# Landmark attention layer: four batch loops against one row of 32 tile slots

## The chip, the cores and the metric

The kernel runs on one core of one Trainium2 chip. The metric is the device time of one execution in microseconds (us). The engines that matter are PE (TensorE, the matrix multiplier), DVE (VectorE), ACT (ScalarE), Pool (GpSimd) and SP (SyncE, which here only issues transfers). Each runs its own instruction list in order; semaphores order them against each other. PEld is the loading of weights into TensorE.

## The reference, cut to what matters

The program computes eight residual layers on x, which has 4 batches of 1024 rows of 128 features: each layer adds f(layernorm(x)) to x. Only the third, the landmark attention, is touched:

```python
def _L0_attn_b_ref(hidden_states, Wq, bq, Wk, bk, Wv, bv):
    L = 64
    q = softmax(hidden_states @ Wq + bq);  k = softmax(hidden_states @ Wk + bk)
    v = hidden_states @ Wv + bv
    k_landmarks = k.reshape(B, L, S // L, D).mean(axis=2)
    kernel_1 = einsum('bqd,bkd->bqk', q, k_landmarks)
    kernel_2 = einsum('bkd,bld->bkl', k_landmarks, k)
    mid = einsum('bkl,bld->bkd', kernel_2, k * v)
    return einsum('bqk,bkd->bqd', kernel_1, mid)
```

The kernel regroups these products. With lm the 64 x 128 landmarks and M = sum over rows of k^T (k * v), a 128 x 128 matrix, the output is q (lm^T lm) M. So a batch needs two sums over its rows (M and lm), then the square lm^T lm, then its product with M, and then q times that.

## The kernel before, in words

`landmark_layer` (lines 827 to 1023) holds x in SBUF (`g.X`, 32 tiles of 128 rows) with the mean and variance of each row (`g.MV`), which the layer before left there. A batch is 8 tiles; a chunk is 4 tiles. All data are f32. The layer opens with three weight and three bias transfers, a square root and reciprocal for the layernorm, and a matrix product that spreads the three biases over all partitions (L914), copied to SBUF by DVE (L971).

Each batch is one call of `sequence` on each engine; three calls are a hardware loop (`Fori`), the fourth is written out. In it:

- PE turns the normalised rows of a chunk (L920); ACT copies them to `xt` (L886). For each tile PE makes q, k and v in one product of 384 columns into one of four PSUM banks (L933). DVE adds the biases in place (L984) and takes the row maxima of q and k (L985). ACT makes both exponentials with their sums (L895, L896). DVE takes the reciprocals of the sums (L990), scales k into `kk` (L992) and makes `k3`, that is k times v (L993). PE adds to M (L938) and to lm (L939) and turns the exponential of q (L944); after four tiles ACT copies the turned ones (L899).
- On PE, tile t's L933 stands ahead of tile t-2's L938, L939 and L944. On DVE, tile t's L984 and L985 stand ahead of tile t-1's L990, L992 and L993.
- At a batch's end, with no tile work of the next one issued yet: DVE copies lm and M (L996, L997), normalises the first chunk of the next batch (L113, four instructions), copies the square (L1001) and the middle product (L1003), adds the eight output tiles to x (L1010), normalises the second chunk, and measures the new x (L122, L125, and a copy of the statistics at L127). PE meanwhile makes the square (L946), turns a chunk, makes the middle product (L950), the eight output tiles in two banks (L955) and turns the second chunk. ACT copies the two turned chunks.

Pool only makes the averaging matrix at the start of this layer. SP has nothing to do after the six transfers. The layers are separated by a barrier of all engines.

## Time and profile before

| | us |
|---|---|
| median of 3 runs | 2824.74 |
| lowest and highest run | 2817.64, 2830.39 |
| the profiled execution: its own time | 2821.07 |
| the profiled execution: span of its trace | 2819.1 |

In that execution PE is busy for 80% of the span, DVE 65%, ACT 51% and Pool 31%, over all eight layers; its mean granted TensorE clock is 0.865 of full speed. The landmark layer is the short stretch from 391.9 to 519.8 us.

How to read the rows further down. Times are us unless marked ns. A row of stretches gives start:end and length, then the busy us (and number of instructions) of PE, PEld, DVE, ACT and Pool in this order, the granted TensorE clock as a share of full speed (0.50 is 1.2 GHz, 1.00 is 2.4 GHz), the share of the DMA engines and the GB/s. A row of a timeline gives the start, the time from the start of the first to the end of the last instruction merged in it, the engine and line, what it writes and reads, shapes and count, and in brackets how long the engine had been idle and what released it. A row of a group gives count, busy us, the mean ns of one, and the idle time ahead of them with its releaser. A line is a line of the kernel before. An f32 matrix product shows as two PE records.

### The profile page before, as it was taken

The page shows a single profiled execution, that of the slowest core. Times are in us where ns is not written, and L with a number is a line of the kernel's source. Part 1 is how long each engine was busy: PE and PEld are TensorE (multiplying, and loading weights), DVE is VectorE, ACT ScalarE, POOL GpSimd, SP SyncE. Part 2 cuts the span into 40 slices and gives each one's busy share as a digit, 9 for nine tenths or more (in the row PEclk, how much of TensorE's full clock was granted, in tenths as well). Part 3 has the DMA queues.
Part 4 walks back from the last instruction along what each step waited for, and adds up shares of the span by engine and source line. Part 5 has one row for each costly group of instructions (what it writes and reads, how often), then busy time and mean ns, then how long its engine had stood idle before and what let it go on. Part 6 is the DMA issues. An engine that isn't in the chain of part 4 may idle for free. (4 is left out here: it accounts for less than half of the span.)

```text
span 2819.1 us, 79607 instructions
## 1 busy us (share of the span) xinstructions
PE 2250.5 (80%) x30676; PEld 1640.9 (58%) x30676; DVE 1820.5 (65%) x5861; ACT 1425.0 (51%) x3583; POOL 865.8 (31%) x852
## 2 busy tenths in 40 slices
PE   6489947589934888798888877948888888888786
PEld 3389924479921333333333337936777777777686
DVE  5533356633335777777777633359999999999533
ACT  4366632366621445445454544635555555555264
POOL 2157620057741100000000002624444444443255
PEclk8589977689965898989989886969999999999688
DMA  3011120011135211111110001121111111111113
GB/s 123 30 38 49 47 68 0 30 35 49 48 126 153 74 32 35 29 30 35 33 43 18 18 3 47 46 84 50 51 50 49 48 50 45 48 48 47 41 39 90
DMA packets 81721, 139.72 MB, mean 50 GB/s; under 512 B 18691, under 2 KB 37803, under 8 KB 78924
## 3 DMA queue, kind: packets, MB, share of 16 engines
q1 hardware_dynamic: 62244, 101.88, 11.6%
q0 software_dynamic: 13824, 28.34, 3.5%
...
q14 instruction: 115, 0.94, 0.1%
...
## 5 line engine op out<-in xcount | busy, mean ns | idle before, releaser
L1353 ACT ACTIVATE ca_pt<-ca_ps 128x512 f32<-128x512 f32 (+3 forms) x768 | 341.1, 491 | 369.6 <-PE ca_ps L1445 168.2
L668 PE MATMUL ffn_ps<-ffn_xst,ffn_up_w 128*128 128x128 f32 x3456 | 430.0, 279 | 0.2 <-issue 0.2
L668 PEld LDWEIGHTS ffn_ps<-ffn_xst,ffn_up_w 128*128 128x128 f32 x3456 | 411.8, 196 | 1.2 <-issue 1.2
L782 DVE TENSOR_TENSOR ffn_hid<-ffn_sg,ffn_ps 128x512 f32<-128x512 f32 x216 | 148.5, 688 | 363.1 <-PE ffn_ps L668 360.2
L540 POOL DMA_INDIRECT ffn_xs<-ffn_x,ffn_token_at x216 | 209.1, 968 | 256.7 <-DVE ffn_token_at L765 192.1
L1419 PE MATMUL ca_ps<-ca_stacks 72*128 72x512 bf16 (+3 forms) x768 | 230.1, 367 | 64.9 <-DVE ca_m_near L1567 31.3
L1774 POOL TENSOR_TENSOR im_pt_e<-im_pt,im_own 128x512 f32<-128x512 f32 x128 | 162.6, 1270 | 384.9 <-DVE im_pt L2027 367.0
L1441 PE MATMUL ca_ps<-ca_stacks 75*128 75x512 bf16 (+3 forms) x768 | 254.0, 354 | 19.2 <-ACT ca_pt L1353 11.2
L1566 DVE TENSOR_REDUCE ca_m_far<-ca_ps 128x1 f32<-128x128 f32 (+5 forms) x384 | 236.6, 616 | 47.1 <-PE ca_ps L1419 45.5
L545 POOL DMA_INDIRECT ffn_y<-ffn_ys,ffn_result_at x216 | 212.6, 984 | 153.7 <-DVE ffn_ys L788 146.1
L1567 DVE CUSTOM_DVE_ANT_0 ca_spill<-ca_ps,ca_bias_q 128x256 f32<-128x256 f32 (+1 forms) x512 | 200.7, 397 | 35.8 <-PE ca_ps L1419 35.8
L1463 PE MATMUL ca_ps<-ca_pt,ca_vp 128*9 128x512 f32 (+3 forms) x1536 | 181.9, 548 | 43.2 <-ACT ca_ysb L1361 43.2
L509 POOL MEMSET ffn_later<- 128x128 f32 x4 | 0.8, 206 | 697.0 <-POOLq L42 697.0
L1781 POOL TENSOR_TENSOR im_rope_qk<-im_t,im_mates 128x512 f32<-128x512 f32 x128 | 170.6, 1333 | 56.8 <-DMA im_mates<-im_t 56.0
L1419 PEld LDWEIGHTS ca_ps<-ca_stacks 72*128 72x128 bf16 x768 | 67.9, 103 | 199.6 <-DVE ca_m_near L1567 100.2
L1580 DVE TENSOR_TENSOR ca_ps<-ca_ps,ca_bias_kd 128x256 f32<-128x256 f32 (+1 forms) x288 | 109.8, 382 | 98.1 <-PE ca_ps L1441 94.6
L1807 ACT ACTIVATE im_ot<-im_ps 128x256 f32<-128x256 f32 x128 | 49.1, 383 | 241.4 <-PE im_ps L1870 241.4
L598 ACT ACTIVATE ffn_up_w<-w_w 128x1024 f32 x144 | 151.9, 1056 | 29.3 <-issue 26.8
L1441 PEld LDWEIGHTS ca_ps<-ca_stacks 75*128 75x128 bf16 x768 | 78.9, 103 | 146.2 <-ACT ca_pt L1353 71.9
L591 ACT ACTIVATE ffn_sg<-ffn_ps 128x512 f32<-128x512 f32 x216 | 128.9, 597 | 59.9 <-PE ffn_ps L668 59.8
L1821 ACT ACTIVATE im_pe_<-im_s,im_nm 128x32 f32<-128x32 f32 x512 | 157.0, 316 | 1.9 <-DVE im_nm L2036 1.9
L676 PE MATMUL ffn_ps<-w_w,ffn_hid 128*128 x1152 | 152.4, 276 | 1.2 <-DVE ffn_ys L788 1.2
...
## 6 DMA issues: line engine op xcount, KB each, us to landing
im_mates<-im_t SPq DMA_DIRECT2D x256, 128.0 KB
...
```

The source lines that it names most:

```text
L540: nc.gpsimd.indirect_dma_start(out=xs[:, n % XS, :], out_offset=None, in_=xn_rows[:, :], in_offset=bass.IndirectOffsetOnAxis(ap=token_at[: ...
L545: nc.gpsimd.indirect_dma_start(out=y_rows[:, :], out_offset=bass.IndirectOffsetOnAxis(ap=result_at[:, n:n + 1], axis=0), in_=ys[:, n % YS, ...
L668: last = nc.tensor.matmul(ps[:, bank, j * P:j * P + P], up_w[:, n % WS, first + j * P:first + j * P + P], xst[:, n % 2, :], start=True, st ...
L1353: nc.scalar.activation(pt[:, i % 8, lo - c0:hi - c0], ps[:, tile_bank(i), lo - c0:hi - c0], ACT.Exp, scale=SCALE).then_inc(p_ready, 1)
L1419: last = nc.tensor.matmul(slot_row(n)[:, c:e], stacks[0:KD, u % 3, 0, j, qt * P:qt * P + P], stacks[0:KD, u % 3, 1, j, c:e], start=True, s ...
L1441: last = nc.tensor.matmul(ps[:, tile_bank(i), lo - c0:hi - c0], stacks[:, u % 3, 1, j, kt * P:kt * P + P], stacks[:, u % 3, 0, j, lo:hi], ...
L1463: nc.tensor.matmul(ps[32 * j:32 * j + D + 1, 7, lo - c0:hi - c0], vp[:, b % 2, kt, gr * G4 + j, :], pt[:, i % 8, lo - c0:hi - c0], start=( ...
L1566: nc.vector.tensor_reduce(m_far[:, u % 2, t:t + 1], slot_row(n)[:, 0:lo], AX_X, ALU.max)
L1567: nc.vector.tensor_tensor_reduce(spill[:, n % 2, 0:hi - lo], slot_row(n)[:, lo:hi], bias_q[:, h, W2 - (hi - lo):W2], 1.0, NEG, ALU.add, AL ...
L1774: nc.gpsimd.tensor_tensor(pt_e[:, j % 2], pt[:].unsqueeze(2).to_broadcast(shape), own[:].unsqueeze(1).to_broadcast(shape), ALU.mult).then_ ...
L1781: nc.gpsimd.tensor_tensor(rope_qk[:, k % 2].rearrange("p a b -> p (a b)"), t1[:], mates[:, k % 2, :], ALU.subtract).then_inc(S["rope_ready ...
L1821: last = nc.scalar.activation(pe_[:, h, :], s1[:, h, :], ACT.Exp, bias=nm[:, h:h + 1], accum_out=sm[:, j % 2, h:h + 1])
```

## The change

The layer becomes one row of 32 tile slots over all four batches, then ten more slots without new tiles. No engine has a hardware loop left in it: everything is written out.

- The work of a batch's end is spread over slots of the next batch. With x the slot's number within a batch, PE: turn the odd chunk at x=1 and the next even one at x=2, square at 3, middle product at 4, first four output tiles at 5, last four at 7. DVE: copies of lm and M at 2, of the square at 3, of the middle product at 4, first four additions to x at 6 and their statistics at 7, the last four at x=0 of the batch after and their statistics at 1. The last batch's end runs in the ten slots without tiles.
- `kk` (L992) goes from DVE to Pool, for all 32 tiles. M's and lm's products now wait for both `k3` from DVE and `kk` from Pool.
- Normalised rows: the first three chunks on DVE at the start, the other 20 tiles on Pool, one after each `kk`.
- Turned x goes through the bank of the output (`ps_o`) and no longer through the bank of the turned exponentials (`ps_t`). Both halves of the output use `ps_o`, so the second waits until the first is added. M and lm share a bank, one bank for each parity of the batch; `xt`, `eqt`, `lm`, `mm`, `aa` and `nn` are doubled, `xn` holds four chunks.
- The spread of the biases no longer waits for the averaging matrix, and the first rows no longer wait for the spread. The statistics are written straight into `g.MV`.

The diff, without the removed lines (they are in the functions above), the declarations of semaphores and unchanged lines; "..." marks what is left out, and eight leading blanks of each line are cut:

```diff
+AHEAD = 3
...
+std, RS = s.sb("std", [P, NT]), s.sb("rstd", [P, NT])
+xn = s.sb("xn", [P, 4, CT, P])
 w = s.sb("w", [P, 3, P])
...
+xt = s.sb("xt", [P, 2, 2, CHUNK])
+nmx, sums, rs = s.sb("nmx", [P, NT, 2]), s.sb("sums", [P, NT, 2]), s.sb("rs", [P, NT, 2])
...
+eqt = s.sb("eqt", [P, 2, TB, P])
+lm, mm, aa, nn = s.sb("lm", [LM, 2, P]), s.sb("mm", [P, 2, P]), s.sb("aa", [P, 2, P]), s.sb("nn", [P, 2, P])
...
 ps_t, ps_qkv, ps_o = s.ps("ps_t", [P, CT, P]), s.ps("ps_qkv", [P, 4, 512]), s.ps("ps_o", [P, CT, P])
...
+ps_sum = s.ps("ps_sum", [P, 2, 512])
...
 mm_ready, a_done, a_ready, n_done, n_ready = (s.sem(n) for n in ("mm_ready", "a_done", "a_ready", "n_done", "n_ready"))
...
+TURN_ODD, TURN_EVEN, MEAN, SQUARE, MIDDLE, OUT0, OUT1 = 1, 2, 2, 3, 4, 5, 7
+def after_slot(n):
+    return n // TB, n % TB
 with nc.Block() as block:
     @block.sync
...
     @block.gpsimd
     def _(pool):
...
+        pool.wait_ge(rstd_ready, 1)
+        pool.wait_ge(xn_ready, AHEAD)
+        def row(n):
+            c, k = n // CT, n % CT
+            if k == 0 and c >= 4:
+                pool.wait_ge(turned, c - 3)
+            last = nc.gpsimd.tensor_scalar(xn[:, c % 4, k, :], g.X[:, n, :], g.MV[:, n, 0:1], RS[:, n:n + 1], ALU.subtract, ALU.mult)
+            if k == CT - 1:
+                last.then_inc(xn_ready, 1)
+        for n in range(NT):
+            pool.wait_ge(rs_ready, n + 1)
+            if n >= 4:
+                pool.wait_ge(summed, n - 3)
+            nc.gpsimd.tensor_scalar(kk[:, n % 4, :], ek[:, n % 4, :], rs[:, n, 1:2], None, ALU.mult).then_inc(kk_ready, 1)
+            if AHEAD * CT + n < NT:
+                row(AHEAD * CT + n)
     @block.scalar
     def _(act):
...
+        nc.scalar.activation(std[:], g.MV[:, :, 1], ACT.Sqrt, bias=g.eps[:, 0:1]).then_inc(std_ready, 1)
+        def copy_xt(c):
+            act.wait_ge(turned, c + 1)
+            nc.scalar.activation(xt[:, c // 2 % 2, c % 2, :], ps_o[:].rearrange("p a b -> p (a b)"), ACT.Copy).then_inc(xt_ready, 1)
+        def exps(n):
+            act.wait_ge(mx_ready, n + 1)
+            if n >= 4:
+                act.wait_ge(summed, n - 3)
+                act.wait_ge(k3_ready, n - 3)
+            nc.scalar.activation(ek[:, n % 4, :], ps_qkv[:, n % 4, P:2 * P], ACT.Exp, bias=nmx[:, n, 1:2], accum_out=sums[:, n, 1:2])
+            nc.scalar.activation(eq[:, n % 4, :], ps_qkv[:, n % 4, 0:P], ACT.Exp, bias=nmx[:, n, 0:1], accum_out=sums[:, n, 0:1]).then_inc(exp_ready, 1)
+        def copy_eqt(k):
+            b, h = k // 2, k % 2
+            act.wait_ge(summed, k * CT + CT)
+            if b >= 2:
+                act.wait_ge(o_ready, 2 * b - 2)
+            nc.scalar.activation(eqt[:, b % 2, h * CT:h * CT + CT, :], ps_t[:], ACT.Copy).then_inc(eqt_ready, 1)
+        copy_xt(0)
+        for n in range(NT + 2):
+            q, x = after_slot(n)
+            if n < NT:
+                exps(n)
+            if n % CT == 1 and n > CT:
+                copy_eqt(n // CT - 1)
+            if x == TURN_ODD and 2 * q + 1 < NC_:
+                copy_xt(2 * q + 1)
+            if x == TURN_EVEN and 2 * q + 2 < NC_:
+                copy_xt(2 * q + 2)
     @block.tensor
     def _(pe):
+        def turn(c):
+            pe.wait_ge(xn_ready, c + 1)
+            for k in range(CT):
+                last = nc.tensor.transpose(ps_o[:, k, :], xn[:, c % 4, k, :], g.ident[:])
+            last.then_inc(turned, 1)
+        def project(n):
+            b, t = n // TB, n % TB
+            if t % CT == 0:
+                pe.wait_ge(xt_ready, 2 * b + t // CT + 1)
+            if n >= 4:
+                pe.wait_ge(k3_ready, n - 3)
+                pe.wait_ge(exp_ready, n - 3)
+            nc.tensor.matmul(ps_qkv[:, n % 4, 0:3 * P], xt[:, b % 2, t // CT, t % CT * P:t % CT * P + P], w[:].rearrange("p a b -> p (a b)"),
+                             start=True, stop=True).then_inc(qkv_ready, 1)
+        def sum_tile(n):
+            b, t = n // TB, n % TB
+            bank = ps_sum[:, b % 2, :]
+            if t == 0 and b >= 2:
+                pe.wait_ge(mm_ready, b - 1)
+            pe.wait_ge(k3_ready, n + 1)
+            pe.wait_ge(kk_ready, n + 1)
+            nc.tensor.matmul(bank[:, 0:P], kk[:, n % 4, :], k3[:, n % 4, :], start=(t == 0), stop=(t == TB - 1), skip_group_check=True)
+            nc.tensor.matmul(bank[0:LM, P:2 * P], avg[:, WIN - PER * t:WIN - PER * t + LM], kk[:, n % 4, :],
+                             start=False, stop=(t == TB - 1), skip_group_check=True)
+            pe.wait_ge(exp_ready, n + 1)
+            if n % CT == 0 and n:
+                pe.wait_ge(eqt_ready, n // CT)
+            nc.tensor.transpose(ps_t[:, n % CT, :], eq[:, n % 4, :], g.ident[:]).then_inc(summed, 1)
+        def square(b):
+            pe.wait_ge(mm_ready, b + 1)
+            if 2 * b + 4 < NC_:
+                pe.wait_ge(xt_ready, 2 * b + 5)
+            elif 2 * b + 3 < NC_:
+                pe.wait_ge(xt_ready, 2 * b + 4)
+            else:
+                pe.wait_ge(x_added, 2 * b)
+            nc.tensor.matmul(ps_o[:, 0, :], lm[:, b % 2, :], lm[:, b % 2, :], start=True, stop=True).then_inc(a_done, 1)
+        def middle(b):
+            pe.wait_ge(a_ready, b + 1)
+            nc.tensor.matmul(ps_o[:, 1, :], aa[:, b % 2, :], mm[:, b % 2, :], start=True, stop=True).then_inc(n_done, 1)
+        def output(b, h):
+            if h == 0:
+                pe.wait_ge(n_ready, b + 1)
+            else:
+                pe.wait_ge(x_added, 2 * b + 1)
+            pe.wait_ge(eqt_ready, 2 * b + h + 1)
+            for k in range(CT):
+                last = nc.tensor.matmul(ps_o[:, k, :], eqt[:, b % 2, h * CT + k, :], nn[:, b % 2, :], start=True, stop=True)
+            last.then_inc(o_ready, 1)
         pe.wait_ge(loaded, 16 * 6)
+        nc.tensor.matmul(ps_sum[:, 1, 0:3 * P], g.ones[0:1, :], brow[:].rearrange("p a b -> p (a b)"), start=True, stop=True).then_inc(spread, 1)
+        turn(0)
...
+        for n in range(NT + TB):
+            q, x = after_slot(n)
+            if n < NT:
+                project(n)
+            if 2 <= n < NT + 2:
+                sum_tile(n - 2)
+            if x == TURN_ODD and 2 * q + 1 < NC_:
+                if q >= 2:
+                    pe.wait_ge(x_added, 2 * q - 2)
+                else:
+                    pe.wait_ge(xt_ready, 2 * q + 1)
+                turn(2 * q + 1)
+            if x == TURN_EVEN and 2 * q + 2 < NC_:
+                pe.wait_ge(xt_ready, 2 * q + 2)
+                turn(2 * q + 2)
+            if q:
+                if x == SQUARE:
+                    square(q - 1)
+                if x == MIDDLE:
+                    middle(q - 1)
+                if x == OUT0:
+                    output(q - 1, 0)
+                if x == OUT1:
+                    output(q - 1, 1)
     @block.vector
     def _(dve):
...
+        dve.wait_ge(std_ready, 1)
+        nc.vector.reciprocal(RS[:], std[:]).then_inc(rstd_ready, 1)
+        dve.wait_ge(rstd_ready, 1)
+        for c in range(AHEAD):
+            for k in range(CT):
+                n = c * CT + k
+                last = nc.vector.tensor_scalar(xn[:, c, k, :], g.X[:, n, :], g.MV[:, n, 0:1], RS[:, n:n + 1], ALU.subtract, ALU.mult)
+            last.then_inc(xn_ready, 1)
+            if c == 0:
+                dve.wait_ge(spread, 1)
+                nc.vector.tensor_copy(bias[:], ps_sum[:, 1, 0:3 * P]).then_inc(spread, 1)
+        dve.wait_ge(spread, 2)
+        def add_bias(n):
+            dve.wait_ge(qkv_ready, n + 1)
+            out = ps_qkv[:, n % 4, 0:3 * P]
+            nc.vector.tensor_tensor(out, out, bias[:], ALU.add).then_inc(biased, 1)
+            dve.wait_ge(biased, n + 1)
+            nc.vector.tensor_reduce(nmx[:, n, :], ps_qkv[:, n % 4, 0:2 * P].rearrange("p (a b) -> p a b", a=2),
+                                    AX_X, ALU.max, negate=True).then_inc(mx_ready, 1)
+        def weigh(n):
+            dve.wait_ge(exp_ready, n + 1)
+            nc.vector.reciprocal(rs[:, n, :], sums[:, n, :]).then_inc(rs_ready, 1)
+            if n >= 4:
+                dve.wait_ge(summed, n - 3)
+            dve.wait_ge(rs_ready, n + 1)
+            nc.vector.scalar_tensor_tensor(k3[:, n % 4, :], ek[:, n % 4, :], rs[:, n, 1:2], ps_qkv[:, n % 4, 2 * P:3 * P],
+                                           ALU.mult, ALU.mult).then_inc(k3_ready, 1)
+        def copy_sums(b):
+            dve.wait_ge(summed, b * TB + TB)
+            nc.vector.tensor_copy(lm[:, b % 2, :], ps_sum[0:LM, b % 2, P:2 * P])
+            nc.vector.tensor_copy(mm[:, b % 2, :], ps_sum[:, b % 2, 0:P]).then_inc(mm_ready, 1)
+        def copy_square(b):
             dve.wait_ge(a_done, b + 1)
...
+            nc.vector.tensor_copy(aa[:, b % 2, :], ps_o[:, 0, :]).then_inc(a_ready, 1)
+        def copy_middle(b):
             dve.wait_ge(n_done, b + 1)
...
+            nc.vector.tensor_copy(nn[:, b % 2, :], ps_o[:, 1, :]).then_inc(n_ready, 1)
+        def add_output(c):
+            dve.wait_ge(o_ready, c + 1)
+            for k in range(CT):
+                n = c * CT + k
+                last = nc.vector.scalar_tensor_tensor(g.X[:, n, :], ps_o[:, k, :], rs[:, n, 0:1], g.X[:, n, :], ALU.mult, ALU.add)
+            last.then_inc(x_added, 1)
+        def new_stats(c):
+            hold(dve, x_added, c + 1)
+            for k in range(CT):
+                last = nc.vector.bn_stats(raw[:, c % 2, k, :], g.X[:, c * CT + k, :])
+            last.then_inc(raw_ready, 1)
+            hold(dve, raw_ready, c + 1)
+            for k in range(CT):
+                nc.vector.bn_aggr(g.MV[:, c * CT + k, :], raw[:, c % 2, k, :])
+        for n in range(NT + TB + 2):
+            q, x = after_slot(n)
+            if n < NT:
+                add_bias(n)
+            if 1 <= n < NT + 1:
+                weigh(n - 1)
+            if q:
+                if x == MEAN:
+                    copy_sums(q - 1)
+                if x == SQUARE:
+                    copy_square(q - 1)
+                if x == MIDDLE:
+                    copy_middle(q - 1)
+                if x == OUT0 + 1:
+                    add_output(2 * q - 2)
+                if x == OUT1:
+                    new_stats(2 * q - 2)
+                if x == 0 and q >= 2:
+                    add_output(2 * q - 3)
+                if x == 1 and q >= 2:
+                    new_stats(2 * q - 3)
 s.clear()
```

## Rows read from the trace of the kernel before

**Rows 1.** Busy time by stretch of this layer: opening, then eight-tile runs and batch ends alternating
```profile
391.90:403.30 11.40, 5.13 (x13) 3.04 (x14) 3.05 (x10) 3.45 (x5) 0.75 (x3) 0.50 0.06 17
403.30:418.40 15.10, 12.93 (x49) 6.28 (x48) 12.67 (x40) 7.56 (x34) 0.00 (x0) 0.94 0.00 1
418.40:431.90 13.50, 9.35 (x39) 6.80 (x39) 8.02 (x38) 3.07 (x4) 0.00 (x0) 0.76 0.00 1
431.90:449.00 17.10, 13.67 (x52) 7.14 (x50) 12.57 (x40) 6.93 (x33) 0.00 (x0) 0.89 0.00 0
449.00:462.40 13.40, 9.33 (x37) 6.26 (x35) 8.02 (x38) 3.07 (x4) 0.00 (x0) 0.77 0.00 0
462.40:478.40 16.00, 12.11 (x46) 6.40 (x45) 12.57 (x40) 6.95 (x33) 0.00 (x0) 0.87 0.00 0
478.40:493.10 14.70, 10.94 (x40) 7.79 (x39) 8.02 (x38) 1.79 (x3) 0.00 (x0) 0.67 0.00 0
493.10:509.50 16.40, 12.30 (x47) 6.38 (x46) 12.57 (x40) 6.94 (x33) 0.00 (x0) 0.88 0.00 0
509.50:519.80 10.30, 4.13 (x26) 3.08 (x25) 6.07 (x30) 0.60 (x1) 0.00 (x0) 0.90 0.00 0
```
**Rows 2.** Timeline of two tiles: start us, us, engine, line, operation, operands, times, idle before
```profile
408.18 0.49 PE L938 MATMUL lm_ps_m<-lm_k,lm_kk 128*128 128x128 f32 x2
...
409.13 0.81 PE L933 MATMUL lm_ps_qkv<-lm_w,lm_xt 128*128 128x384 f32 x2
...
409.99 0.56 DVE L984 TENSOR_TENSOR lm_ps_qkv<-lm_ps_qkv,lm_bias 128x384 f32<-128x384 f32 x1
...
410.65 0.42 DVE L985 TENSOR_REDUCE lm_nmx<-lm_ps_qkv 128x2 f32<-128x256 f32 x1
...
410.99 0.16 DVE L990 RECIPROCAL lm_rs<-lm_sums 128x2 f32<-128x2 f32 x1
...
411.25 0.29 DVE L992 TENSOR_SCALAR lm_kk<-lm_ek,lm_rs 128x128 f32<-128x128 f32 x1
...
411.45 0.34 DVE L993 SCALAR_TENSOR_TENSOR lm_k<-lm_ek,lm_rs,lm_ps_qkv 128x128 f32<-128x128 f32 x1
```
**Rows 3.** Timeline of the end of the last batch
```profile
510.64 0.28 DVE L996 COPY lm_lm<-lm_ps_lm 64x128 f32<-64x128 f32 x1 [1.20 <-PE lm_ps_t L944]
...
511.18 0.49 PE L946 MATMUL lm_ps_o<-lm_lm 64*128 64x128 f32 x2 [0.57 <-DVE lm_mm L997]
...
512.92 1.16 PE L955 MATMUL lm_ps_o<-lm_nn,lm_eqt 128*128 128x128 f32 x8 [0.38 <-DVE lm_nn L1003]
...
514.12 1.13 DVE L1010 SCALAR_TENSOR_TENSOR g_x<-lm_ps_o,lm_rs,g_x 128x128 f32<-128x128 f32 x4 [1.25 <-PE lm_ps_o L955]
...
516.38 0.87 DVE L122 BATCH_NORM_STATS2 lm_raw<-g_x 128x6 f32<-128x128 f32 x4
517.35 0.38 DVE L125 BATCH_NORM_AGGREGATE g_mv<-lm_raw 128x2 f32<-128x6 f32 x4
```
**Rows 4.** Timeline: opening of the layer, and a turn with its copy at full clock
```profile
395.24 1.61 PE L914 MATMUL lm_ps_lm<-lm_brow,g_ones 1*128 1x384 f32 x2 [33.64 <-DMA lm_brow<-in_L_attn_b_bv_dram]
...
403.30 0.57 DVE L984 TENSOR_TENSOR lm_ps_qkv<-lm_ps_qkv,lm_bias 128x384 f32<-128x384 f32 x1 [2.49 <-PE lm_ps_qkv L933]
...
421.20 0.66 PE L920 MATMUL lm_ps_t<-g_ident,lm_xn 128*128 128x128 f32 x4 [0.61 <-DVE lm_xn L113]
...
421.89 0.60 ACT L886 ACTIVATE lm_xt<-lm_ps_t 128x512 f32<-128x512 f32 x1 [1.73 <-PE lm_ps_t L920]
```
**Rows 5.** Groups of Pool instructions, by form: count, busy us, mean ns, idle before
```profile
L1291 POOL TENSOR_SCALAR ca_xn<-g_x,g_mv,ca_rstd 128x128 f32<-128x128 f32 x24 | 18.8, 793 | 269.6 <-ACT ca_xt L1316 269.6
L190 POOL TENSOR_TENSOR ssm_t<-ssm_zg,ssm_rows 128x512 f32<-128x512 f32 x8 | 14.9, 1862 | 0.6
...
L186 POOL TENSOR_TENSOR ssm_zg<-ssm_z,ssm_rows 128x512 f32<-128x512 f32 x8 | 10.1, 1263 | 62.5 <-ACT ssm_z L248 62.5
...
L513 POOL TENSOR_SCALAR_AFFINE_SELECT ffn_later<-ffn_later 128x128 f32<-128x128 f32 x4 | 1.2, 292 | 0.3
```

More of the change, by code:

```diff
@@ L841, in landmark_layer @@
         avg = s.sb("avg", [P, WIN + LM])
-        xt = s.sb("xt", [P, 2, CHUNK])
-        nmx, sums, rs = s.sb("nmx", [P, TB, 2]), s.sb("sums", [P, TB, 2]), s.sb("rs", [P, TB, 2])
+        xt = s.sb("xt", [P, 2, 2, CHUNK])
+        nmx, sums, rs = s.sb("nmx", [P, NT, 2]), s.sb("sums", [P, NT, 2]), s.sb("rs", [P, NT, 2])
         eq, ek = s.sb("eq", [P, 4, P]), s.sb("ek", [P, 4, P])
@@ L881, in _ @@
+                for n in range(NT):
[5 more added lines that the diff above has]
+                        row(AHEAD * CT + n)
             @block.scalar
             def _(act):
-                norm.act_std(act)
-                def copy_xt(b, h):
-                    act.wait_ge(turned, b * 2 + h + 1)
-                    nc.scalar.activation(xt[:, h, :], ps_t[:].rearrange("p a b -> p (a b)"), ACT.Copy).then_inc(copied, 1)
@@ L888, in sequence @@
-                def sequence(b, last):
-                    for t in range(TB + 2):
-                        n = b * TB + t
-                        if t < TB:
-                            act.wait_ge(mx_ready, n + 1)
-                            act.wait_ge(k3_ready, n + 1)
-                            act.wait_ge(acc_done, n + 1)
-                            nc.scalar.activation(ek[:, t % 4, :], ps_qkv[:, t % 4, P:2 * P], ACT.Exp, bias=nmx[:, t, 1:2], accum_out=sums[:, t, 1:2])
-                            nc.scalar.activation(eq[:, t % 4, :], ps_qkv[:, t % 4, 0:P], ACT.Exp, bias=nmx[:, t, 0:1], accum_out=sums[:, t, 0:1]).then_inc(exp_ready, 1)
-                        if t in (5, 9):
-                            act.wait_ge(acc_done, n + 3)
-                            nc.scalar.activation(eqt[:, t - 5:t - 1, :], ps_t[:], ACT.Copy).then_inc(copied, 1)
-                    if not last:
-                        copy_xt(b + 1, 0)
-                        copy_xt(b + 1, 1)
@@ L903, in _ @@
-                copy_xt(0, 0)
-                copy_xt(0, 1)
-                with act.Fori(0, BATCH - 1) as b:
-                    sequence(b, False)
-                sequence(BATCH - 1, True)
+                nc.scalar.activation(std[:], g.MV[:, :, 1], ACT.Sqrt, bias=g.eps[:, 0:1]).then_inc(std_ready, 1)
+                def copy_xt(c):
+                    act.wait_ge(turned, c + 1)
+                    nc.scalar.activation(xt[:, c // 2 % 2, c % 2, :], ps_o[:].rearrange("p a b -> p (a b)"), ACT.Copy).then_inc(xt_ready, 1)
@@ L912, in _ @@
+                turn(0)
                 pe.wait_ge(made, 3)
-                pe.sem_inc(acc_done, 4)
-                nc.tensor.matmul(ps_lm[:, 0:3 * P], g.ones[0:1, :], brow[:].rearrange("p a b -> p (a b)"), start=True, stop=True).then_inc(spread, 1)
-                pe.wait_ge(spread, 2)
-                def turn(b, h):
-                    pe.wait_ge(xn_ready, b * 2 + h + 1)
-                    pe.wait_ge(copied, b * 4 + h + 1)
-                    for k in range(CT):
-                        t = nc.tensor.transpose(ps_t[:, k, :], norm.xn[:, k, :], g.ident[:])
-                    t.then_inc(turned, 1)
@@ L959, in _ @@
-                turn(0, 0)
-                turn(0, 1)
-                with pe.Fori(0, BATCH - 1) as b:
-                    sequence(b, False)
-                sequence(BATCH - 1, True)
+                for n in range(NT + TB):
[22 more added lines that the diff above has]
+                            output(q - 1, 1)
@@ L1002, in sequence @@
+                def copy_middle(b):
                     dve.wait_ge(n_done, b + 1)
-                    nc.vector.tensor_copy(nn[:], ps_o[:, 1, :]).then_inc(n_ready, 1)
-                    for h in range(2):
-                        c = b * 2 + h
-                        dve.wait_ge(o_ready, c + 1)
-                        for k in range(CT):
-                            t = h * CT + k
-                            xk = tile_of(g.X, b * TB + t)
-                            add = nc.vector.scalar_tensor_tensor(xk, out_bank(h, k), rs[:, t, 0:1], xk, ALU.mult, ALU.add)
-                        add.then_inc(x_added, 1)
@@ L1012, in sequence @@
-                    if not last:
-                        normalise(b + 1, 1)
-                    hold(dve, x_added, b * 2 + 2)
-                    for h in range(2):
-                        ch.link(dve_new_stats(nc, dve, g, raw, b * 2 + h, ch))
-                    assert ch.n == STEPS, ch.n
-                normalise(0, 0)
-                normalise(0, 1)
-                with dve.Fori(0, BATCH - 1) as b:
-                    sequence(b, False)
-                sequence(BATCH - 1, True)
+                    nc.vector.tensor_copy(nn[:, b % 2, :], ps_o[:, 1, :]).then_inc(n_ready, 1)
```

89 lines of the change are left out of this document (7 added, 82 removed).

## The prediction

> **What bounds the kernel now.** I read the page first for the share of this layer, then the busy time by stretch inside it, then the timeline of two tiles and of a batch's end, and last the Pool groups of the whole kernel. The layer is 127.9 us of a 2819.1 us span, and a barrier stands on either side, so what is saved inside it is saved whole and nothing else moves. It has an opening of 11.4 us, four runs of eight tiles (15.1, 17.1, 16.0 and 16.4 us), three batch ends between them (13.5, 13.4 and 14.7 us) and a last end of 10.3 us [rows 1]. The reader is to see two limits there.
>
> In a tile run it is a loop through PE and DVE: from the start of the product into M (408.18) by the next projection (409.13), the bias (409.99), the maxima (410.65), the reciprocal (410.99), kk (411.25) and k3 (411.45, ends 411.79) [rows 2]; with the same step of 0.05 to PE that is 3.66 us. It spans two tiles, since PE's projection runs one tile ahead: 1.83 us a tile. PE itself has 12.93 busy of 15.10 us, ACT 7.56 [rows 1]. From the products of PE, 0.95 from the start of one tile's sums to the next projection and about 0.81 for that, I take 1.72 of PE work a tile at full clock.
>
> In a batch's end it is a chain of short steps in which PE, DVE and ACT wait for each other: in the second, 9.33 us of PE and 8.02 of DVE in 13.4 us [rows 1]. Behind each end the granted TensorE clock is low: 0.76, 0.77 and 0.67 in the ends (a mix of 1.2 and 2.4 GHz) and 0.87 to 0.89 in the tile runs that follow them, against 0.94 in the first [rows 1].
>
> **The change part by part.**
>
> *The plain tile slot.* DVE loses kk: the reciprocal comes 1.00 after the bias starts, k3 ends 0.60 later, so the slot costs DVE 1.65 with the step to the next. The path to the sums of PE gets longer, since they now wait for kk from Pool. No Pool instruction of kk's form, one tensor and one scalar per row, is in the trace. Its bounds: 0.29 us (Pool's affine select on the same shape) and 1.17 us (793 ns of Pool's row normalisation, a tensor with two scalars per row, times 1862/1263, by which one Pool operation outlasts its twin of the same shape in the first layer) [rows 5]. I take 0.79, the same operation with one scalar more. With 0.16 for the reciprocal and 0.1 for the semaphore, reciprocal to kk is 1.05 us, where reciprocal to the end of k3 was 0.80: the loop grows from 3.66 to 3.91, a plain slot from 1.83 to 1.96. At the bounds it is 1.80 (k3's 0.60 is then the longer path) and 2.15. Pool's pair of kk and row costs 1.6 us a slot and fits; at 1.17 each it would be 2.34 and set the plain slots.
>
> *What the slots carry.* DVE: additions of four tiles 1.13; their statistics 0.87 and 0.38 with the two waits 1.45; lm and M 0.5; copies of square and middle 0.25 to 0.3 each [rows 3]. PE: a turn 0.66 [rows 4], square and middle 0.45 and 0.40, four output tiles 1.06 to 1.16 [rows 3]. Per batch DVE has 8 x 1.65 + 6.2 = 19.4 us, PE 8 x 1.72 + 4.3 = 18.1, ACT 8 x 1.1 + 4 x 0.6 = 11.3 [rows 1, 4], Pool 12.6. The sum per batch lies near both DVE and PE, so I walk an inner batch slot by slot. A bias starts at the later of: the bias before it + 1.65 + DVE's load of that slot; the bias two before + 2.10 + 1.81 + PE's load (kk, then sums and projection); PE's end of the last projection + 1.81 + its load.
>
> From x=0: 2.78 (additions on DVE), 3.10 (statistics on DVE; PE's turn waits until 3.05 and is not last), 2.15 (DVE copies; PE's even turn waits at about 6.2 for ACT, which has two exponentials and two copies to do, and stays 0.3 ahead), 2.2 (square, PE last), 2.2 (middle, PE), 2.9 (first output, PE), 2.78 (DVE), 3.10 (DVE; the second output waits for the additions and ends 0.9 ahead). Sum 21.2 us, against 16.0 + 14.7 = 30.7 for a run and an end now. Batch 1 has no additions at x=0 and 1; there the turns on PE decide and the same walk gives 20.3.
>
> *Opening.* The spread ends at 396.85 [rows 4]; the turn follows at once (its rows were ready at 395.1), at 1.2 GHz 1.1 us, then copy 0.6 and projection 1.4: first bias 400.2 in place of 403.3. But the turns of slots 1 and 2 and ACT's copy now stand between the first tiles; by the walk slot 4 starts at 408.8 where it was 409.99, and with plain slots of 1.96 slot 8 starts at 416.6. The removed second wait thus gives about 1 us, not 3.
>
> *The last end.* Additions and statistics of batch 2's last chunk (2.6 us) now stand ahead of the copies of the sums; 1.2 of it lies in what was DVE's wait for PE [rows 3]. The chain copy, square, copy, middle, copy, output stays. The output's second half now waits for the first additions, but DVE does their statistics meanwhile (1.45 against 1.16 of PE), so it is not late. Two copies of statistics go (0.35 with their wait, each). From slot 32 I get 11.9 us, of which 0.6 is the last k3.
>
> *Sum.* Opening to the first bias 8.3, slots 0 to 8 16.4, then 20.3, 21.2, 21.2, then 11.9: 99.3 us against 127.9, so 28.6 less. The profiled execution took 2821.07, and would take 2792.5; it lies 3.7 below the median shown, and on the median the sum gives 2796.1. I say 2796.
>
> *Edits at nothing.* Doubled buffers and the parity banks cost no instruction. The hardware loop goes; its back edge hides in PE's projections now, and three ACT table loads of 1.3 us lay in the same cover, so their loss gains nothing. 20 row normalisations leave DVE; their cost on Pool is hidden because they run three chunks ahead; 12 stay in DVE's opening, before 399.7, in the cover of the turn and the projection. Without that cover they would cost 1.1 us a chunk. No DMA moves.
>
> *A rule against this.* Pool's row here takes 793 ns and DVE's 0.27 to 0.29 for the same shape [rows 2, 5]. The Trainium skill, "GPSIMD Engine Reference", section "Engine selection", tells one to keep elementwise work on VectorE, GpSimd being about half as fast with two inputs and near line rate with one. By "about half as fast" kk would be some 0.55 us and the plain slot 1.84, an estimate from that page; by the row it is 1.96. The trace has the operation at 2.8 times, so I go by the row.
>
> **The rivals.**
>
> *The clock falls anyway.* PE would have waits of up to 1.2 us at x=0 to 2 (about 4.3 busy of 6.2 us). Now each end and the run behind it have about 2 x 0.24 x 13.5 + 2 x 0.11 x 17.1 = 10 us at 1.2 GHz [rows 1]. If the same 10 us stayed in each of three batches, with PE near its bound, each loses about 5: 2796 + 15 = 2811. Against it: the clock fell behind ends with PE 70% busy and chains of waits for over 10 us; it was 0.94 in a run with PE 86% busy [rows 1], and the new batch has 18.1 of 21.2, or 85%, without an end.
>
> *Pool is slow beside DVE.* Price: at 1.17 us an operation, 8 plain slots x 0.4 and 1 us a batch, about 6 us: 2802. The case on the other side is the same mechanism further on: the place is the first 20 slots, where kk of a tile queues behind the row before it. The 28.6 us are used up when these 20 slots take 3.6 us each or so, a Pool operation of 1.8 us; at 2.1 us they take 4.2, the other 12 about 2.65, and the layer 8 + 84 + 32 + 12 = 136 us: 2833, slower. For it: the twin that takes 1.47 times as long. Against: the 24 rows of this very form have a mean of 793 [rows 5] and would have to go to 2.6 times.
>
> The Trainium skill, "SBUF — State Buffer", section "Who interferes with whom", says that a DVE instruction blocks GpSimd only if it has two SBUF inputs or is in a mode that takes both ports. By that rule the case would not come, as bias, k3 and additions each have one input in PSUM; no row here tests it beside such a load.
>
> *DVE and PE overlap better.* The walk may count a wait twice; if each inner batch reached DVE's own 19.4 us and the plain slots 1.80, that is 2 + 2 x 1.8 + 1.3 = about 7 less: 2789.
>
> *The change does little*, because a wait of the new order that I don't see (the shared output bank, the copy of ACT before the square) is late by 1 to 2 us in each turn of it: 5 places in three batches, 15 us or more: 2811 to 2820.
>
> **How the numbers follow.** Forecast with its neighbours Pool at 1.17 and better overlap (2786 to 2805): 0.72. Clock 0.12, unseen wait 0.10, Pool so slow that the kernel is slower or equal 0.06, of which 0.04 slower. Measurement spread on the median of three is some 5 us, about half a per cent is what can be told from no change; that is 14 us, so the border is 2810.6. Faster: all of the 0.72, half of the clock case, a little of the rest: 0.80. Same 0.15, slower 0.05. The range: 2785 (better overlap less the spread) to 2812 (takes in the clock case).
>
> **What the trace will show.** No gap of PE over 2 us between the first projection and slot 32; the layer some 99 us long; slots 3 to 8 at 1.9 to 2.0 us from bias to bias; inner batches of 21 us with PE and DVE both at 80% or more; the clock 0.95 or more behind the opening; Pool's kk and rows near 0.8 us; what PE's product into M waits for in plain slots is Pool's kk. I am wrong if Pool's kk is above 1.2 us or below 0.5, if the clock is under 0.9 in an inner batch, or if one slot of the eight is over 4 us.

## The result, and the profile after

| | before | after |
|---|---|---|
| median | 2823.26 us (4 runs) | 2789.14 us (4 runs, 2778.68 to 2797.55) |
| ratio of times | | 0.9891, 95% interval 0.9855 to 0.9927 |
| span of the profiled execution | 2819.1 us | 2776.7 us |
| landmark layer, from its first table load on ACT to that of the next layer | 128.8 us | 95.1 us |

The median fell by 34.1 us; 28.6 were forecast, 2796 on the median, and the range was 2785 to 2812. The two spans differ by 42.4 us, which is more than the change did. The edges of the layer are one ACT instruction each, in the timeline of ACT, first before, then after:

```profile
391.88 1.28 ACT L102 ACT_TABLE_LOAD   x1 [11.23 <-PEq L42]
...
520.64 1.28 ACT L567 ACT_TABLE_LOAD   x1 [9.40 <-PEq L42]
```
```profile
388.92 1.28 ACT L904 ACT_TABLE_LOAD   x1 [11.91 <-PEq L42]
...
483.98 1.28 ACT L567 ACT_TABLE_LOAD   x1 [12.36 <-PEq L42]
```

520.64 - 391.88 = 128.76 and 483.98 - 388.92 = 95.06, so the layer gave 33.7 us in the two profiled executions. The other 8.7 us of the spans are other layers. Taken between the first Pool instructions of the layers, the seventh took 787.7 us in the profile before and 774.9 after, and 758.9 to 786.8 in the kernels below, none of which touches it; the fifth took 863.0 to 879.9. The landmark layer itself repeats: the changed kernel once more, on a chip where the second and third layer with experts took 320 and 181 us in place of 299 and 172, gave 94.99. From here on I compare the layer. There is one profile of the kernel before, and its last end ran at a higher clock than the same instructions did in another kernel (see unrolled), which made it some 2 us shorter.

Busy time by stretch after (columns as in [rows 1]): slots 0 to 7, then three batches of eight slots, then the tail.

```profile
397.50:411.95 14.45, 13.07 (x54) 7.10 (x53) 10.73 (x31) 7.66 (x34) 8.69 (x13) 0.91 0.00 0
411.95:430.30 18.35, 17.19 (x88) 10.74 (x88) 14.04 (x49) 8.79 (x39) 12.26 (x18) 1.00 0.00 1
430.30:449.60 19.30, 16.80 (x85) 10.25 (x84) 16.00 (x62) 8.42 (x36) 8.79 (x13) 1.00 0.00 1
449.60:468.90 19.30, 15.77 (x80) 9.57 (x79) 15.92 (x62) 7.92 (x35) 4.83 (x8) 1.00 0.00 1
468.90:484.00 15.10, 7.14 (x27) 5.32 (x26) 8.50 (x44) 0.62 (x2) 0.63 (x2) 0.59 0.00 1
```

The batch ends of [rows 1] are gone. From slot 8 on the clock is 1.00, PE is busy for 17.19 of 18.35 us, then 16.80 and 15.77 of 19.30, and DVE for 14.04, 16.00 and 15.92. Only the tail falls back to 1.2 GHz; its 0.59 is a mix of both levels. No wait of PE between the first projection and the tail exceeds 1.0 us.

The timeline of two plain tiles, to be read against [rows 2]:

```profile
404.98 0.46 PE L962 MATMUL lm_ps_sum<-lm_k,lm_kk 128*128 128x128 f32 x2 [0.50 <-POOL lm_kk L898]
...
405.90 0.81 PE L952 MATMUL lm_ps_qkv<-lm_w,lm_xt 128*128 128x384 f32 x2
...
406.75 0.57 DVE L1041 TENSOR_TENSOR lm_ps_qkv<-lm_ps_qkv,lm_bias 128x384 f32<-128x384 f32 x1 [0.75 <-PE lm_ps_qkv L952]
...
407.35 0.42 DVE L1043 TENSOR_REDUCE lm_nmx<-lm_ps_qkv 128x2 f32<-128x256 f32 x1
...
407.69 0.15 DVE L1048 RECIPROCAL lm_rs<-lm_sums 128x2 f32<-128x2 f32 x1
...
407.94 0.61 POOL L898 TENSOR_SCALAR lm_kk<-lm_ek,lm_rs 128x128 f32<-128x128 f32 x1 [0.83 <-DVE lm_rs L1048]
407.95 0.35 DVE L1052 SCALAR_TENSOR_TENSOR lm_k<-lm_ek,lm_rs,lm_ps_qkv 128x128 f32<-128x128 f32 x1
```

The loop from the product into M (404.98) to the end of kk is still there and has not become shorter. The reciprocal starts at 407.69, kk on Pool at 407.94 and ends at 408.55; k3 on DVE ended at 408.30. Two tiles take 3.71 us (bias at 403.03, 406.75, 410.46), against 3.66.

A slot that DVE sets, the first of the third batch:

```profile
430.33 0.54 DVE L1041 TENSOR_TENSOR lm_ps_qkv<-lm_ps_qkv,lm_bias 128x384 f32<-128x384 f32 x1
430.91 0.42 DVE L1043 TENSOR_REDUCE lm_nmx<-lm_ps_qkv 128x2 f32<-128x256 f32 x1
431.25 0.15 DVE L1048 RECIPROCAL lm_rs<-lm_sums 128x2 f32<-128x2 f32 x1
431.51 0.35 DVE L1052 SCALAR_TENSOR_TENSOR lm_k<-lm_ek,lm_rs,lm_ps_qkv 128x128 f32<-128x128 f32 x1
431.77 1.12 DVE L1072 SCALAR_TENSOR_TENSOR g_x<-lm_ps_o,lm_rs,g_x 128x128 f32<-128x128 f32 x4
432.81 0.55 DVE L1041 TENSOR_TENSOR lm_ps_qkv<-lm_ps_qkv,lm_bias 128x384 f32<-128x384 f32 x1
```

From bias to bias 2.48 us, each instruction following the one before without a gap; before, the first additions of an end stood behind a wait of 1.25 to 2.36 us for PE.

Pool's two operations and the product that waits for kk, by form:

```profile
L898 POOL TENSOR_SCALAR lm_kk<-lm_ek,lm_rs 128x128 f32<-128x128 f32 x32 | 19.4, 607 | 44.8 <-DVE lm_rs L1048 41.8 <-PE lm_ps_t L968 2.7
...
L890 POOL TENSOR_SCALAR lm_xn<-g_x,g_mv,lm_rstd 128x128 f32<-128x128 f32 x20 | 16.1, 806 | 0.0
L962 PE MATMUL lm_ps_sum<-lm_k,lm_kk 128*128 128x128 f32 x64 | 13.9, 300 | 9.3 <-POOL lm_kk L898 9.0
```

### The profile page after: what moved, and what is told of

It reads as the page before. It is cut to its first block and busy times, and to the rows that moved or that the text cites. A ratio compares the mean times of both kernels' runs of the same rounds, so it can differ in the third digit from the quotient of the medians.

```text
span 2776.7 us, 79320 instructions
## 1 busy us (share of the span) xinstructions
PE 2235.6 (81%) x30676; PEld 1627.3 (59%) x30676; DVE 1800.7 (65%) x5801; ACT 1423.3 (51%) x3581; POOL 903.3 (33%) x904
```

## The experiments

Theory S: the gain is the overlap of the batch ends with tile work. Rivals: P, the relief of DVE by Pool; H, the hardware loops and their waits. Layer lengths below are from table load to table load, as above, each from the one profiled execution of its kernel.

**serial_ends.** All of the change but the spreading; PE's part of the edit, condensed (ACT and DVE alike):

```diff
-for n in range(NT + TB):        # project(n), sum_tile(n - 2), and parts of batch q - 1 by x
+for b in range(BATCH):
+    for t in range(TB + 2): ... # project, sum_tile
+    turn(2 * b + 2); square(b); middle(b); output(b, 0); output(b, 1); turn(2 * b + 3)
```

> All of the change but the spreading: no hardware loops, kk and rows on Pool, shared output bank, direct statistics, but each batch's end stands alone between the tile runs. Measure: the layer from its first table load on ACT to that of the next layer, 128.8 us before and 95.1 after. Theory S (the gain is the overlap of the ends with tile work): three ends of 12 to 14 us come back, layer 120 to 130 us, total about 2815 to 2825. Rival P (relief of DVE by Pool makes the gain): layer 110 or less, total 2805 or less. Rival H (the hardware loops and their waits cost it): the same, 110 or less.

Measured: layer 131.2 us, just above the 120 to 130 of S; total 2812.95, ratio 0.9942 (0.9905 to 0.9979). In the total some gain is left, in the layer none: it is 2.5 us longer than before. So what is left in the total lies in other layers. DVE's timeline at the first batch's end:

```profile
421.80 0.29 DVE L1053 COPY lm_aa<-lm_ps_o 128x128 f32<-128x128 f32 x1 [1.24 <-PE lm_ps_o L976]
422.98 0.29 DVE L1057 COPY lm_nn<-lm_ps_o 128x128 f32<-128x128 f32 x1 [0.89 <-PE lm_ps_o L980]
425.44 1.12 DVE L1063 SCALAR_TENSOR_TENSOR g_x<-lm_ps_o,lm_rs,g_x 128x128 f32<-128x128 f32 x4 [2.17 <-PE lm_ps_o L989]
428.74 1.13 DVE L1063 SCALAR_TENSOR_TENSOR g_x<-lm_ps_o,lm_rs,g_x 128x128 f32<-128x128 f32 x4 [2.17 <-PE lm_ps_o L989]
...
432.35 0.56 DVE L1032 TENSOR_TENSOR lm_ps_qkv<-lm_ps_qkv,lm_bias 128x384 f32<-128x384 f32 x1
```

This is the chain of [rows 3] again, now with the second output waiting for the first additions: the two sets of additions start 3.30 us apart (425.44, 428.74), where they started 1.36 apart in the first end before:

```profile
424.76 1.13 DVE L1010 SCALAR_TENSOR_TENSOR g_x<-lm_ps_o,lm_rs,g_x 128x128 f32 x4 [2.36 <-PE lm_ps_o L955]
426.12 1.12 DVE L1010 SCALAR_TENSOR_TENSOR g_x<-lm_ps_m,lm_rs,g_x 128x128 f32 x4 [0.24 <-PE lm_ps_m L955]
```

In all four ends it is 3.3 us in place of 1.36, 1.70, 1.70 and 1.04: where the ends are not spread, the shared bank costs 7.4 us. From the last bias of a batch to the first of the next it is 16.7, 18.1 and 17.5 us, against 16.9, 16.9 and 17.5 before. The clock is back at 1.2 GHz as well, in the stretch from the last statistics into the next run:

```profile
430.00:436.00 6.00, 5.29 (x12) 2.96 (x12) 5.33 (x24) 2.21 (x9) 1.17 (x2) 0.50 0.02 4
```

The 110 us or less of P and H did not come, so the spreading makes most of the gain. It doesn't make all of it: this run also pays the 7.4 us of the shared bank, which the spread kernel hides. Without them the layer would take some 124 us (an estimate, 131.2 - 7.4), about 5 less than before, for all the other edits together.

**no_pool.** The spreading with kk and rows on DVE:

```diff
 def weigh(n):                                     # DVE
+    nc.vector.tensor_scalar(kk[:, n % 4, :], ek[:, n % 4, :], rs[:, n, 1:2], None, ALU.mult)
...
         weigh(n - 1)
+        if AHEAD * CT + n - 1 < NT:
+            row(AHEAD * CT + n - 1)               # was Pool's
```

> The spreading with nothing on Pool: kk and the 20 row normalisations go back to DVE, one row in each of slots 1 to 20. DVE gets 0.20 us more a slot for kk and 0.26 for a row. Theory S: only slots set by DVE pay (four of eight in inner batches), plain slots gain 0.06 by the shorter way to kk: layer 95.1 + 3 to 6 = 98 to 101 us, total about 2794. Rival P: DVE becomes the limit in nearly all slots, 32 x 0.2 + 20 x 0.26 = 11.6 us, layer 107, total about 2801.

Measured: layer 97.6 us; total 2773.97, ratio 0.9847 (0.98 to 0.9894). That is at S's 98 to 101 and far from P's 107. The slot above, the first of the third batch, with kk and a row on DVE:

```profile
431.27 0.54 DVE L1022 TENSOR_TENSOR lm_ps_qkv<-lm_ps_qkv,lm_bias 128x384 f32<-128x384 f32 x1
...
432.44 0.29 DVE L1033 TENSOR_SCALAR lm_kk<-lm_ek,lm_rs 128x128 f32<-128x128 f32 x1
432.65 0.34 DVE L1034 SCALAR_TENSOR_TENSOR lm_k<-lm_ek,lm_rs,lm_ps_qkv 128x128 f32<-128x128 f32 x1
432.90 0.34 DVE L1041 TENSOR_SCALAR lm_xn<-g_x,g_mv,lm_rstd 128x128 f32<-128x128 f32 x1
433.16 1.12 DVE L1062 SCALAR_TENSOR_TENSOR g_x<-lm_ps_o,lm_rs,g_x 128x128 f32<-128x128 f32 x4
434.20 0.55 DVE L1022 TENSOR_TENSOR lm_ps_qkv<-lm_ps_qkv,lm_bias 128x384 f32<-128x384 f32 x1
```

It takes 2.93 us where the change has 2.48; the seventh slot of that batch, with kk but no row left to make, takes 2.70 where the change has 2.51. By the forecast's prices 11.6 us of work went back to DVE, and the layer grew by 2.6: most of the work fell into time that PE set. So of the 33.7 us Pool gives 2.6, and 31.1 are there with nothing of the layer's tile work on Pool. With the opening, which keeps 2.5 us (below), that leaves some 28.6 for the spreading. This split is worked out from the runs; no run has the opening's edit alone.

**kk_on_dve.** Only kk goes back, rows stay on Pool (first line of the diff above).

> The changed kernel with kk on DVE again, rows still on Pool. Reciprocal to kk and k3 on DVE is 0.15 + 0.11 + 0.20 + 0.35 and 0.06 to PE, 0.87 us, where by Pool it is 0.26 + 0.61 and 0.14, 1.01 us. Theory S: plain slots 1.79 in place of 1.855 us, DVE-set slots 0.20 longer, four in an inner batch: layer 95.1 - 1 + 2 = 95 to 97 us. Rival P: 32 x 0.2 = 6.4 more, 101 us.

Measured, in one run: layer 95.75 us, 0.7 more than the change. Slots 0 to 8 take 14.07 in place of 14.41, the third batch 19.86 in place of 19.31: kk on Pool helps where DVE sets the pace and hurts where the loop does, and the two nearly cancel. The rows are worth the other 1.9.

**unrolled.** The kernel before, with `Fori` written as a Python loop on ACT, PE and DVE, and nothing else.

> The kernel before with its three hardware loops written out and nothing else changed. Theory S: layer 127 to 129 us, as before 128.8. Rival H: waits on register values and back edges cost in every tile, layer 120 or less.

Measured, in one run: layer 130.2 us, 1.4 longer than before and above the 127 to 129 expected. The excess is in the last end, whose instructions are the same as before. Its stretch, and PE's first output in it:

```profile
509.50:519.80 10.30, 5.44 (x21) 4.49 (x20) 5.25 (x24) 0.60 (x1) 0.00 (x0) 0.67 0.00 0
```
```profile
512.50 2.08 PE L955 MATMUL lm_ps_o<-lm_nn,lm_eqt 128*128 128x128 f32 x8 [0.38 <-DVE lm_nn L1003]
```

Before, the clock there was 0.90 and the output took 1.16 [rows 1, 3]. From the last bias to the next layer it is 16.2 us against 14.0; all that stands ahead of it takes 114.0 against 114.8. So the loops cost 0.8 us at most, and H falls. (Its total, 2805.54, is 17 below the median before while its layer is 1.4 longer: the seventh layer took 758.9.)

**nops.** Where the forecast had a DVE slot too long:

```diff
-dve.wait_ge(biased, n + 1)
+hold(dve, biased, n + 1)        # the wait, then an empty instruction
...
-dve.wait_ge(rs_ready, n + 1)
+hold(dve, rs_ready, n + 1)
```

> The changed kernel with the two waits inside a slot on DVE (bias to maxima, reciprocal to k3) written as before, with an empty instruction behind the wait. Theory N (these took 0.06 us each and were the reason that a DVE slot costs 1.44 us and not 1.65): bias to maxima 0.66 in place of 0.60, reciprocal to k3 0.32 in place of 0.26; DVE-set slots 0.12 longer, plain ones 0.03; layer 95.1 + 2 to 3 = 97 to 98 us. Rival (the shorter steps come from waits on constants in place of registers): no change, 95 us.

Measured, in one run: layer 95.8, 0.8 more and not the 2 to 3 expected. DVE's timeline, bias to maxima:

```profile
426.41 0.56 DVE L1041 TENSOR_TENSOR lm_ps_qkv<-lm_ps_qkv,lm_bias 128x384 f32<-128x384 f32 x1
427.07 0.42 DVE L1043 TENSOR_REDUCE lm_nmx<-lm_ps_qkv 128x2 f32<-128x256 f32 x1
```

0.66 in place of 0.60; but the reciprocal to k3 stayed at 0.26; a second wait stands there anyway, which may be why (not tested). So one of the two empty instructions costs 0.06, DVE-set slots grew by 0.05 to 0.07 and not by 0.12, and theory N holds for the one and not for the other.

**warm.** For the tail:

```diff
+def spend(k, cols):             # a product that nobody reads
+    nc.tensor.matmul(ps_qkv[:, k, 0:cols], g.ident[:], ..., start=True, stop=True)
+for k in range(18): spend(k % 4, P)               # ahead of the wait for the loads
...
+if n in (NT, NT + 1): spend(0, 2 * P)
...
+if q == BATCH: spend(0, 3 * P)                    # behind output(q - 1, 0)
```

> The changed kernel with added products on PE whose results nobody reads: 18 of 128 columns before the loads land, one of 256 columns in each of slots 32 and 33, one of 384 behind the first output of the last batch. Theory C (the tail's excess over the forecast, 13.9 against 11.9 us, is the clock at 1.2 GHz): square and middle 0.5 in place of 0.8 us, outputs 1.1 in place of 2.08 each, tail 2 us shorter; the opening up to the first bias 1 to 2.5 us shorter if the clock rises before the spread. Layer 95.1 - 2 to 4.5 = 91 to 93 us. Rival D (the tail is long because statistics and additions of the chunk before stand ahead of it on DVE): the tail stays within 0.5 us whatever the clock.

Measured, in one run: layer 94.5, where 91 to 93 were expected; from the last bias to the next layer 16.30 us in place of 17.76; D's half microsecond is exceeded and C holds for 1.5 of its 2 us. PE in the tail (square, first and second outputs):

```profile
498.10 0.48 PE L978 MATMUL lm_ps_o<-lm_lm 64*128 64x128 f32 x2 [1.01 <-DVE lm_mm L1067]
...
499.84 2.03 PE L991 MATMUL lm_ps_o<-lm_nn,lm_eqt 128*128 128x128 f32 x8 [0.38 <-DVE lm_nn L1075]
...
503.09 1.26 PE L991 MATMUL lm_ps_o<-lm_nn,lm_eqt 128*128 128x128 f32 x8
```

The square takes 0.48 as at full clock, but the clock fell again inside the first output (2.03) and the second shows 1.26. The opening got 1.1 us longer, where 1 to 2.5 shorter was expected. PE's timeline there:

```profile
413.71 6.30 PE L995 MATMUL lm_ps_qkv<-g_x,g_ident 128*128 128x128 f32 x36 [30.79 <-PEq L42]
419.94 0.91 PE L1000 MATMUL lm_ps_sum<-lm_brow,g_ones 1*128 1x384 f32 x2
```

18 products took 6.30 us and the loads had landed after some 3.4, so the true spread started late, though it then took 0.91 in place of 1.64.

**best.** As warm, with the statistics of chunk 5 at x=4 of the tail in place of x=1.

> The kernel with the added products, and the statistics of the last chunk of batch 2 moved from slot 33 to slot 36, behind the copy of the last middle product. By theories C and D both: the chain of the last batch starts about 0.9 us sooner and the statistics lie in DVE's wait for the first output (2.1 us at 1.2 GHz, 1.2 at full clock). Layer another 0.7 us below that of the added products alone, 90 to 92 us.

Measured, in one run: layer 93.3, where 90 to 92 were expected; from the last bias to the next layer 14.54, another 1.8 (the opening was 0.6 longer than in warm, so the layer shows 1.2 of it). Only half of the 1.8 is the order on DVE. The copy of lm starts 4.81 us after the last bias where it was 5.72 in warm; from there to the first additions it is 3.47 in place of 4.31, because the clock held. PE in the two outputs:

```profile
500.73 1.16 PE L991 MATMUL lm_ps_o<-lm_nn,lm_eqt 128*128 128x128 f32 x8 [0.38 <-DVE lm_nn L1075]
...
503.10 1.16 PE L991 MATMUL lm_ps_o<-lm_nn,lm_eqt 128*128 128x128 f32 x8 [0.57 <-DVE g_x L1081]
```

So the new order gives 0.9 us and the clock another 0.8. No run has the new order without the added products.

**best_mix.** As best, with kk split by slot:

```diff
+ON_POOL = [n for n in range(TB, NT) if (n + 1) % TB in (6, 7) or (n + 1) % TB in (0, 1) and n > 2 * TB - 2]
```

> The same, with kk on DVE in slots that PE sets and on Pool in those that DVE sets (tiles weighed at x=6 and 7 of each batch from the second, and at x=0 and 1 from the third). By the two routes' lengths (0.87 us on DVE, 1.01 by Pool) plain slots gain up to 0.07 and DVE-set slots lose nothing: layer 1 us below the same kernel with all kk on Pool, 89 to 91 us; total about 4 us below the changed kernel's 2789, too little to tell, 0.986 of before. If DVE's extra 0.20 us counts in the PE-set slots after all, no gain.

Measured: layer 90.5. Slots 0 to 8 take 13.72 against 14.17, the three batches 17.98, 19.08 and (seven slots) 16.37 against 18.38, 19.31 and 16.60, where best has kk on Pool throughout. The split gives these 1.3 us of the 2.8 between the two layers; the rest is opening and tail, whose instructions are the same (9.21 us to the first bias against 10.29, 14.18 behind the last against 14.54). Total 2848.75 against 2886.87 before on the same chip, ratio 0.987 (0.9837 to 0.9903).

**after_again and best_mix10.** The changed kernel once more, and best_mix with `range(10)` in the opening, on one chip.

> The changed kernel once more, beside the next on the same chip. If the other layers make the difference between the total times of kernels and the landmark layer repeats, its length is 95.1 us within 0.5, and the total 33 to 35 us below the kernel before, ratio 0.987 to 0.989.

> The last kernel with 10 added products ahead of the loads in place of 18. The 18 took 6.3 us and held the first true product back by some 2.8 us; 10 at the same 0.35 us end with the loads. If the clock rises by then, the first bias comes 7 to 7.5 us after the layer's start in place of 9.2 (8.6 with none), layer 88 to 89.5 us; if it rises later, 8.2 to 8.6 and layer about 90. Total 38 to 41 us below before, ratio about 0.986; against the changed kernel 0.998, not to be told from one.

Measured: after_again 94.99 us for the layer, as expected, but ratio 0.9847 (0.9816 to 0.9877), where 0.987 to 0.989 was expected: the median fell by 46.9 us against the kernel before on that chip, some 13 more than the layer's 33.7. What gave them is not shown; the kernel before has no profile there. best_mix10 89.7, ratio 0.9835 (0.9821 to 0.9849); first bias 7.51 us after the layer's start (8.56 with no added products). PE's opening:

```profile
415.40 4.08 PE L998 MATMUL lm_ps_qkv<-g_x,g_ident 128*128 128x128 f32 x20 [31.20 <-PEq L42]
419.41 0.91 PE L1003 MATMUL lm_ps_sum<-lm_brow,g_ones 1*128 1x384 f32 x2
```

The spread took 0.91 us, as in warm, and the granted clock from 419.37 on is 1.00. In warm, best and best_mix, with the same 18 products ahead, the first bias came 9.73, 10.29 and 9.21 us after the layer's start; the clock rose at different times in them. The tail was 0.9 us longer than best_mix's with the same instructions. The same stretch of best_mix, then of best_mix10, by busy time:

```profile
497.00:500.00 3.00, 2.29 (x12) 1.49 (x12) 2.31 (x13) 0.00 (x0) 0.00 (x0) 1.00 0.03 5
```
```profile
497.00:500.00 3.00, 2.90 (x10) 2.07 (x10) 2.12 (x13) 0.00 (x0) 0.00 (x0) 0.55 0.00 0
```

The clock is 1.00 in the one and 0.55 in the other: the added products don't hold it there reliably, and what decides it is not shown. Totals 2840.32 and 2839.52 us can't tell the two kernels apart; the layer can, 5.3 us.

## Why the prediction was right

The number was right (2796 against 2789.14), and so was the mechanism: the ends vanish into the slots, and nothing else of size happens. Part of the match is luck: the slots came out 7.7 us shorter than forecast and the tail 2.0 longer, so the layer alone gave 33.7 us and not 28.6; and that the median fell by 34.1, close to the layer, is chance as well, since it fell by 46.9 on another chip. By its own steps, in us:

| step | forecast | measured |
|---|---|---|
| opening to first bias | 8.3 | 8.6 |
| slots 0 to 8 | 16.4 | 14.4 |
| second batch | 20.3 | 18.4 |
| third batch | 21.2 | 19.3 |
| fourth batch | 21.2 | 19.3 |
| tail | 11.9 | 13.9 |
| sum to the last statistics | 99.3 | 93.9 |

- *Kk on Pool*: 0.79 taken, 0.607 measured, within the bounds 0.29 and 1.17. It starts 0.25 after the reciprocal's start and PE follows 0.14 after its end, so it is the longer path, as forecast; a plain slot takes 1.855, forecast 1.96. Of the forecast's two prices, 0.79 by the row and the 0.55 that it turned down, the second was the nearer. Two of its sums are off without touching the result: at a kk of 0.29 the loop would be 3.46 and the plain slot 1.73, not 1.80, and the 28.6 us would be used up at 3.8 us in each of the 20 slots, not 3.6.
- *The DVE slot*: 1.65 taken, 1.44 measured. This is the term that was mis-sized most: the four slots that DVE sets are 1.35 of the 1.9 us by which the third batch came out shorter. I had added the whole of k3 (0.34) and a step, but the next DVE instruction starts 0.26 after k3's start (431.51, 431.77): that is 0.13. The empty instruction behind the bias, which the rows before still had, is 0.06 more, as nops shows. In the same way additions cost 1.04 and not 1.13, statistics 1.26 and not 1.45. [rows 2] already had it: kk to k3 there is 0.20 between starts, with kk 0.29 long.
- *Slot by slot* in the third batch: 2.48, 2.71, 1.84, 2.46, 1.71, 2.89, 2.51, 2.71 against 2.78, 3.10, 2.15, 2.2, 2.2, 2.9, 2.78, 3.10. The four slots named as DVE's are, and x=5 with its output is PE's and exact.
- *The opening*: the first bias came 8.62 us after the layer's start, against 11.42 before, as forecast. That the turns of slots 1 and 2 would eat most of it was too gloomy: slot 4 starts at 15.6 us (404.52 - 388.92) against 18.1 (409.99 - 391.88), so 2.5 us are kept and not about 1.
- *The tail*: the only step of size that came out longer. Statistics and additions of chunk 5 stood ahead of the chain as forecast, but the clock was 1.00 until 471.1 and 0.50 from 472.4 on, after PE had idled for 1.44 us. The forecast had priced the chain from [rows 3], the one end before that ran at 2.4 GHz (0.90 over its stretch, 0.67 to 0.77 in the three others); unrolled shows the same end at 1.2. The stretch of square and middle product by busy time, and the timeline:

```profile
472.40:474.70 2.30, 1.59 (x4) 1.00 (x4) 0.56 (x2) 0.00 (x0) 0.00 (x0) 0.50 0.00 0
```
```profile
471.93 0.25 DVE L1057 COPY lm_lm<-lm_ps_sum 64x128 f32<-64x128 f32 x1
...
472.43 0.79 PE L978 MATMUL lm_ps_o<-lm_lm 64*128 64x128 f32 x2 [1.44 <-DVE lm_mm L1058]
...
474.78 2.08 PE L991 MATMUL lm_ps_o<-lm_nn,lm_eqt 128*128 128x128 f32 x8 [0.38 <-DVE lm_nn L1066]
476.90 1.12 DVE L1072 SCALAR_TENSOR_TENSOR g_x<-lm_ps_o,lm_rs,g_x 128x128 f32<-128x128 f32 x4 [2.17 <-PE lm_ps_o L991]
...
478.12 0.87 DVE L1078 BATCH_NORM_STATS2 lm_raw<-g_x 128x6 f32<-128x128 f32 x4
```

Square 0.79 and output 2.08 against 0.49 and 1.16 in [rows 3]. From this kernel to best the tail lost 3.2 us: 2.3 from the copies of the sums on, where only the clock differs in what the chain waits for, and 0.9 ahead of them, which is the order on DVE. The clock alone thus covers the forecast's 2.0.

- *The clock rival* was right that the clock would fall and wrong about the place: 1.00 in all inner batches, 0.59 in the tail. In serial_ends, where the ends are back, the stretch behind an end shows it at 0.50 again. How much of the 33.7 us is clock and how much is waiting was not measured apart.
- *Pool beside DVE*: all 32 kk took 602 to 622 ns and all 20 rows 804 to 808, with DVE busy for 74 to 83% of the stretches in which they ran. The slower rival had no ground. By the rule of the Trainium skill, "SBUF — State Buffer", section "Who interferes with whom", a DVE instruction with at most one input in SBUF, outside the modes that take both ports, doesn't contend with GpSimd; the trace agrees, with kk at 602 to 622 ns. The factor 1.47, from which I took my upper bound, is that of L190 in the first layer: 2.06 us in the six cases beside a scan on DVE with two inputs in SBUF, 1.26 in the two without one. That same rule would have told them apart.
- *Edits at nothing* cost next to nothing: the loops 0.8 us at most (unrolled), and the shared bank once the ends are spread, for no output of an inner batch waits for the additions before it. In the tail it does, for 1.22 us.
- *Signs that failed*: slots 3 to 8 at 1.9 to 2.0 us (1.86), inner batches of 21 (18.4 and 19.3), DVE at 80% in each (77% in the second batch), kk near 0.8. All are the sizes above; none of the signs of being wrong came.
